# Routing of the last batch placed inside the expert block, expert weights in ten parts, a scan for the running sums

## The reference

```python
x = x + attn_a(norm(x))      # 16 heads, random features, and a dense feed-forward part
x = x + ffn(norm(x))         # 160 experts, the stage called m in the kernel
x = x + attn_b(norm(x))      # causal, 16 heads of 8, four sequences
x = x + ffn(norm(x))         # 160 experts again, the stage called n
...
# ffn, for every token
probs = sigmoid(x @ router_w.T + expert_bias)          # [T, 160]
top_w, top_idx = top_k(probs, 8)
top_w = 2.5 * top_w / (sum(top_w) + 1e-9)
combine[t, top_idx] = top_w
h1 = silu(einsum('th,eih->eti', x, w_gate))            # w_gate [160, 64, 128]
routed = einsum('eti,ehi->th', h1 * combine, w_down)   # w_down [160, 128, 64]
shared = silu(x @ w_gate_shared.T) @ w_down_shared.T
out = routed + shared
```

## Time and profile before

| | us |
|---|---|
| time before, median of 3 runs | 2836.28 |
| lowest and highest of them | 2828.25, 2845.3 |
| the profiled execution, its own time | 2840.0 |
| its span, first to last instruction | 2838.8 |
| around the span | 1.2 |
| mean granted TensorE clock | 0.806 of full |

### The profile page before, as it was taken

How to read it: one execution, slowest core, us unless ns; L and a number is a source line. 1 busy time by engine, 2 the same in 40 slices (tenths; PEclk the granted TensorE clock), 3 DMA queues, 4 the chain that set the end, 5 groups by cost and what they waited for, 6 DMA issues and landing times. The chain is left out here.

```text
span 2838.8 us, 45747 instructions
## 1 busy us (share of the span) xinstructions
PE 2002.9 (71%) x15915; PEld 1145.2 (40%) x15915; DVE 1632.1 (57%) x4701; ACT 1087.8 (38%) x2067; POOL 1264.2 (45%) x1244
## 2 busy tenths in 40 slices
PE   5898887877882775665878889888888467676000
PEld 3456455455461554542333333333342255454000
DVE  5457585784777231457776878688783533145222
ACT  0263453453540443440545544443444144444000
POOL 0043166566673444543434420430443444456775
PEclk8899989999995897885787878787887589878555
DMA  9200001000034664554132130121100656555221
GB/s 377 95 1 4 1 6 35 24 12 34 19 131 154 195 209 158 186 177 123 29 90 50 48 82 21 50 74 33 50 29 26 252 182 211 181 187 175 70 59 45
DMA packets 132475, 275.70 MB, mean 97 GB/s; under 512 B 29411, under 2 KB 44387, under 8 KB 127891
## 3 DMA queue, kind: packets, MB, share of 16 engines
q1 hardware_dynamic: 99478, 205.60, 21.8%
q0 software_dynamic: 32768, 67.17, 7.8%
HBM read 146.34 MB, written 125.93 MB: 96 GB/s over the span
## 5 line engine op out<-in xcount | busy, mean ns | idle before, releaser
L1473 POOL DMA_INDIRECT slots_in<-g_xs,g_place x512 | 508.5, 993 | 500.7 <-ACT b_pT L2521 188.6
L2521 ACT ACTIVATE b_pT<-b_psE 128x512 f32<-128x512 f32 (+3 forms) x768 | 330.4, 491 | 469.6 <-PE b_psE L2420 228.9
L2271 DVE TENSOR_REDUCE b_peak<-b_psM 128x1 f32<-128x512 f32 (+3 forms) x768 | 394.5, 551 | 141.5 <-PE b_psM L2403 87.0
L1498 POOL DMA_INDIRECT r_xs<-slots_out,g_place x336 | 333.0, 991 | 312.4 <-ACT b_pT L2521 183.3
L2400 PE MATMUL b_psM<-b_kS,b_qS 72*128 72x512 bf16 (+3 forms) x768 | 283.9, 402 | 66.2 <-DVE b_peak L2271 34.0
L2416 PE MATMUL b_psE<-b_qS,b_kS 75*128 75x512 bf16 (+3 forms) x768 | 258.5, 391 | 57.1 <-ACT b_pT L2521 39.5
L1498 POOL DMA_INDIRECT g_xs<-slots_out,g_place x176 | 172.4, 980 | 124.4 <-issue 48.1
L2060 DVE COPY m_staged_w<-wgd 128x192 f32 x512 | 98.3, 263 | 222.5 <-PE m_psY L2002 114.5
L2060 DVE COPY n_staged_w<-wgd 128x192 f32 x512 | 97.8, 262 | 207.7 <-PE n_psY L2002 147.8
L2430 PE MATMUL b_psV<-b_pT,b_vb 128*32 128x512 f32 (+3 forms) x1536 | 197.3, 597 | 2.5 <-ACT b_pT L2521 2.2
L2400 PEld LDWEIGHTS b_psM<-b_kS,b_qS 72*128 72x128 bf16 x768 | 83.5, 111 | 264.7 <-DVE b_peak L2271 138.6
(11 more groups left out here) (640 smaller groups left out, 4167.3 us busy)
## 6 DMA issues: line engine op xcount, KB each, us to landing
wgd<-in_w_gdT SPq DMA_DIRECT2D x8, 3840.0 KB, 23.0
slots_in<-g_xs SPq DMA_DIRECT2D x26, 1024.0 KB
m_rows<-slots_in SPq DMA_DIRECT2D x104, 256.0 KB
slots_out<-m_y SPq DMA_DIRECT2D x104, 256.0 KB
n_rows<-slots_in SPq DMA_DIRECT2D x104, 256.0 KB
slots_out<-n_y SPq DMA_DIRECT2D x104, 256.0 KB
b_qS<-q_parts SPq DMA_DIRECT2D x48, 192.0 KB
b_kS<-k_parts SPq DMA_DIRECT2D x48, 192.0 KB
```

Source lines behind the costliest of these rows:

```text
L1473: self.nc.gpsimd.indirect_dma_start(self.G.slots_in[self.h], bass.IndirectOffsetOnAxis(self.G.place[:, TPH * self.h + t, k:k + 1], 0), sel ...
L1498: self.nc.gpsimd.indirect_dma_start(self.rows(i)[:, k, :], None, self.G.slots_out[t // TPH], bass.IndirectOffsetOnAxis(self.G.place[:, t, ...
L2271: nc.vector.reduce_max(to, taking()[:, 0:size], AX.X).then_inc(m_taken, 1)
L2521: nc.scalar.activation(pT[:, e % KEPT, h, q0:HALF], psE[:, j % BANKS, q0:HALF], ACT.Exp, scale=SCALE).then_inc(e_taken, 1)
```

## The change

- `route` is gone. Its instructions for the last batch stand in `experts`, beside the 20 fixed groups of the first half. `Beside` says after which group each part of PE and ACT comes: in m (`LOADED_BESIDE_FFN`) turn after group 0, score 1, up 2, down 3, count 8, rank 9, owner 16; in n (`ALL_LOADED_HERE`) turn before group 0, score 0, up 1, down 2, count 3, rank 4, owner 10.
- DVE does the whole routing first, then waits for all weights, then begins to stage.
- The first half runs its 20 fixed groups first and its 32 dynamic ones after them (`static_first`; in m it begins with fixed group 10). The second half keeps `group_order`.
- While the routing uses the second psum banks, the fixed groups use the first one alone (`alone`), so `up(n)` waits for `squash(n-1)` and `down(n)` for `take_y(n-1)`.
- Buffers of the routing lie in the staging buffers (`Carved`).
- Weights come in 10 parts of 1.57 MB. In m five come during `ffn_a` and five beside groups 0, 2, 4, 6, 8. In n two come between the first four row loads and eight beside groups 0 to 14.
- POOL sends the rest of batch 2 at three transfers a group from the start, and then, once the slots are known (`placed`), batch 3 at two a group from group 19 on.
- The running sum is one `tensor_tensor_scan` in place of a copy and 8 doubling steps.

```diff
-CHUNKS = 4
+CHUNKS = 10
...
+def static_first(first):
+    return [((first + i) % STATIC_GROUPS, None) for i in range(STATIC_GROUPS)] + [(STATIC_GROUPS + d, d) for d in range(DYN_GROUPS)]
...
-def route(nc, stage, G, W, h, first, tiles, xn, xn_free=None, send=None, loads=None):
...
+LOADED_BESIDE_FFN = Beside(STATIC_GROUPS // 2, range(CHUNKS // 2), 0, 2, turn=0, score=1, up=2, down=3, count=8, rank=9, owner=16)
+ALL_LOADED_HERE = Beside(0, range(CHUNKS), 2, 2, turn=-1, score=0, up=1, down=2, count=3, rank=4, owner=10)
...
+        def alone(n):
+            return n < STATIC_GROUPS
...
+            def load_chunk(c):
+                e = slice(CHUNK * c, CHUNK * (c + 1))
+                sp.dma_start(G.wgd[:, e, :], W["w_gdT"][:, e, :]).then_inc(S.weights_landed[c], 16)
...
                 for i in range(DEEP):
-                    load(h, i)
+                    load(first + i)
+                    if h == 0 and i == 1:
+                        sp.dma_start(wr, W["routerT"]).then_inc(router_landed, 16)
...
+                    if h == 0 and 1 <= i <= beside.upfront:
+                        load_chunk(chunks.pop(0))
                 for i in range(HALF_GROUPS):
                     if i + DEEP < HALF_GROUPS:
-                        sp.wait_ge(x_turned, h * HALF_GROUPS + i + 1)
-                        load(h, i + DEEP)
-                    store(h, i)
+                        sp.wait_ge(x_turned, first + i + 1)
+                        load(first + i + DEEP)
+                    if chunks and i % beside.per == 0:
+                        load_chunk(chunks.pop(0))
+                    store(first + i)
...
-            spaced(scatter, TPH * TOPK - scatter.sent, 0, 3, 2)
+            scatter.upto = TPB * TOPK
+            spaced(scatter, TPB * TOPK - scatter.sent, 0, 3, 1)
+            scatter.of_batch(BATCH - 1)
+            pool.wait_ge(placed, 1)
+            spaced(scatter, TPB * TOPK, STATIC_GROUPS - 1, 2, 1)
...
+                if n and alone(n - 1):
+                    pe.wait_ge(hT_ready, n)
...
+                if n and alone(n - 1):
+                    pe.wait_ge(y_ready, n)
...
             for h in range(HALVES):
                 first = h * HALF_GROUPS
                 turn_rows(first)
-                for i, (g, d) in enumerate(order):
-                    up(first + i, g, d, h * DYN_GROUPS)
+                if h == 0:
+                    last_batch_at(-1)
+                for i in range(HALF_GROUPS):
+                    up(first + i)
                     if i + 1 < HALF_GROUPS:
                         turn_rows(first + i + 1)
                     if i:
-                        down(first + i - 1, *order[i - 1])
...
+                        down(first + i - 1)
+                    if h == 0:
+                        last_batch_at(i)
...
+            def last_batch_at(i):
+                if i == beside.turn:
+                    for u, ps in enumerate((bank0, bank1)):
+                        act.wait_ge(turned, u + 1)
+                        nc.scalar.activation(xnT[:, u * HALF:(u + 1) * HALF], ps, ACT.Copy).then_inc(xnT_ready, 1)
+                if i == beside.score:
+                    act.wait_ge(logits_taken, 1)
+                    nc.scalar.activation(probs, logits, ACT.Sigmoid).then_inc(probs_ready, 1)
+                if i == beside.up:
+                    for u, ps in enumerate(ups):
+                        act.wait_ge(up_shared, 2)
+                        nc.scalar.activation(hs[:, u * HALF:(u + 1) * HALF], ps[0:INTER, :], ACT.Silu).then_inc(hs_ready, 1)
...
-                step, now = 1, 0
-                while step < EXPERTS:
-                    nc.vector.tensor_copy(ends[:, 1 - now, 0:step], ends[:, now, 0:step])
-                    nc.vector.tensor_tensor(ends[:, 1 - now, step:], ends[:, now, step:], ends[:, now, 0:EXPERTS - step], ALU.add)
...
+                nc.vector.tensor_tensor_scan(ends, more, more, 0.0, ALU.add, ALU.max)
...
+            norm()
+            dve.wait_ge(made, 1)
...
+            add_bias()
+            choose()
+            for u in range(2):
+                add_shared(u)
+            plan()
+            find_places()
+            order_weights()
+            write_owners()
             for c in range(CHUNKS):
                 dve.wait_ge(S.weights_landed[c], 16)
             for d in range(DYN_GROUPS):
                 stage_weights(0, d)
+            dve.wait_ge(owners_written, 1)
...
-                route(nc, "m3_", G, W, *part(BATCH - 1), send, expert_loads(G, W, S["m"], range(CHUNKS // 2)))
-                send.of_batch(BATCH - 1)
-                experts(nc, "m", G, S["m"], send)
+                experts(nc, "m", G, W, S["m"], send, part(BATCH - 1), LOADED_BESIDE_FFN)
```

More of the change, by code:

```diff
@@ L1892, in experts, with __init__ @@
-def experts(nc, stage, G, S, scatter, out=None):
+class Beside:
+    def __init__(self, first_group, chunks, upfront, per, turn, score, up, down, count, rank, owner):
+        self.first_group, self.chunks, self.upfront, self.per = first_group, list(chunks), upfront, per
+        self.turn, self.score, self.up, self.down, self.count, self.rank, self.owner = turn, score, up, down, count, rank, owner
+LOADED_BESIDE_FFN = Beside(STATIC_GROUPS // 2, range(CHUNKS // 2), 0, 2, turn=0, score=1, up=2, down=3, count=8, rank=9, owner=16)
@@ L1896, in experts @@
+def experts(nc, stage, G, W, S, scatter, last_batch, beside, out=None):
+    h_last, first_tile, tiles, xn, xn_free = last_batch
+    assert tiles == TPB and first_tile == TPB and h_last == HALVES - 1
     with Memory(nc, stage) as m:
@@ L1927, in _ @@
             for h in range(HALVES):
+                first = h * HALF_GROUPS
                 for b in range(BPH * h, BPH * (h + 1)):
@@ L1949, in spaced @@
                 for n in range(0, count, transfers):
-                    done = min(n // transfers * groups, HALF_GROUPS)
+                    done = min(n // transfers * groups, HALF_GROUPS - first % HALF_GROUPS)
                     if done:
@@ new lines, in count, with rank @@
+            def count():
+                pe.wait_ge(made, 3)
+                pe.wait_ge(picked_ready, 1)
+                nc.tensor.matmul(counts, ones_bf, before[:, TPB, :], start=True, stop=True).then_inc(counted, 1)
+            def rank():
+                pe.wait_ge(share_ready, 1)
+                pe.wait_ge(shared_taken, 2)
+                for tiles_here, ps in rank_tiles:
+                    if tiles_here.stop == TPB:
+                        pe.wait_ge(count_taken, 1)
+                    for i, t in enumerate(range(tiles_here.start, tiles_here.stop)):
+                        nc.tensor.matmul(ps[:, i, :], earlier, picked[:, t, :], start=True, stop=False)
+                        nc.tensor.matmul(ps[:, i, :], ones_bf, before[:, t, :], start=False, stop=False)
+                        last = nc.tensor.matmul(ps[:, i, :], ones_bf[0:1, :], share[:], start=False, stop=True)
+                last.then_inc(ranked, 1)
@@ new lines, in turn_owner @@
+            def turn_owner():
+                pe.wait_ge(owner_ready, 1)
+                pe.wait_ge(rank_taken, 1)
+                for i in range(OWNERS):
+                    last = nc.tensor.matmul(owners[:, i * P:(i + 1) * P], owner[:, i:i + 1], G.ident[:], start=True, stop=True)
+                last.then_inc(owner_turned, 1)
+            def last_batch_at(i):
+                if i == beside.turn:
+                    turn_last_batch()
+                if i == beside.score:
+                    score()
+                if i == beside.up:
+                    up_of_shared()
+                if i == beside.down:
+                    down_of_shared()
+                if i == beside.count:
+                    count()
+                if i == beside.rank:
+                    rank()
+                if i == beside.owner:
+                    turn_owner()
```

588 lines of the change are left out of this document (250 added, 338 removed).

## The result

The changed kernel took 2815.1 us, the median of six runs (2804.2 to 2821.5), against 2837.1 for the kernel before (six runs, 2828.3 to 2845.3). The ratio is 0.9926, with a 95% interval of 0.9898 to 0.9954. It is faster by 22 us, where 72 were forecast, and lies outside the range. That of before is 2.9 above its own.

What follows compares the result with a forecast made beforehand. DVE's serial chain was taken to bound the routing blocks, and PE's loop the groups. Terms of -42.3 us in m and -30.2 in n took 2840.0 to 2767.5; the stated median was 2765, the 8-in-10 range 2745 to 2800.

Steps and rivals of the forecast that it cites:

- Staging: First halves' 32 dynamic groups in a row: DVE's staging takes 2.1 us against 2.98 a group, so it costs nothing.
- Routing beside the groups, +18 and +16: First halves' fixed groups: the routing work of PE and ACT adds 18 us in m and 16 in n.
- parts, +2 and +4: Weight parts loaded beside the fixed groups: mostly absorbed by rows asked for ahead, costing 2 us in m and 4 in n.
- The round trip of ACT: After the scores, ACT waits for DVE's bias, then does a table load and sigmoid before the next squash: 4.0 us exposed.
- +3.7 for `up(0)` in n: Start of n: group 0 needs weight part 0, so its up starts at about 9.5 us in place of 5.8.
- Gap between m's halves, -8.4: Between m's halves: row copies start in time, so the gap of 8.9 us shrinks to n's 0.5.
- Slots known at 65 and 52 us: Batch 3's slots known 65 us into the block in m and 52 in n, before group 19's result at some 83.
- Bounds: Whole kernel: 2745 us with full clock for PE's parts (-11), DMA absorbed and ACT's trip half hidden; 2814 the other way.
- The first: Rival: DMA bounds the fixed groups, late rows stopping the loop; +17 over the terms, 2782 us; chance 0.14.
- The second: Rival: each of PE's routing parts stops the loop, which starts anew; +30, 2795 us; chance 0.13.
- The third: Rival: slots known only after group 31, so copies end 35 us after the last result; 2835 us; chance 0.03.
- Staging (0.04): Rival: staging bounds the dynamic groups in a row; slower by over 0.5% from 4.35 us a group; chance 0.04.

Runs made afterwards that it cites:

- e2: Changed kernel with the last batch's 64 row copies moved behind the first half's last result; with its three repeats 2709 to 2721 us, before at 2607 to 2613.
- e4: Kernel before with the changed kernel's order in the first halves, fixed groups first and then 32 dynamic ones, copies still three for two groups; ratio 0.9990 to before.
- e14: Changed kernel with the last batch's copies released from the 12th result on in place of the 20th; ratio 0.9800 to before.
- e13: Changed kernel with n's last eight weight parts asked for one to a group in place of one to two groups; ratio 0.9855 to before.

## Why the prediction was wrong

**The failed step is the cost of the row copies beside the groups.** The prediction put it as "At two per group they need 2.5 us of 2.98", a claim on POOL's time alone, and under Staging as "Nothing": 2.98 us was kept as the pace of a dynamic group, while the change raises the rate from 1.5 copies a group to 2. Measured in the comparison: the dynamic groups of m carried 62 copies where before's last 32 groups carried 48, and took 15.0 us longer; those of n carried 62 in place of 42 and took 16.9 longer. That is 1.07 and 0.85 us for each copy more, near the 0.96 for which a copy keeps POOL busy. The row that said so stood in the prediction's own material: the second halves, with two gathers a group, take 191 us for 52 groups in the earlier trace rows, 3.48 each in n between first and last result, where the first halves take 2.98. I read their length as given and never asked why a group costs half a microsecond more there.

Behind it stands a count that I left out. The routing block hid 20 copies a stage (20.60 us of POOL in the earlier trace rows). When the block goes, they move beside the groups, in n all of them beside the dynamic ones. In the sum they were free.

**How firmly this stands.** That order and staging are not the cause is shown by e2 and its repeats and by e4, at the lower level. For the comparison it rests on its own traces: PE never waits for DVE in the dynamic groups, and before runs fixed groups at 2.9 to 3.0 us with DVE idle. That copies beside the loop lengthen it is shown at both levels: in the comparison by before's groups with three copies and with none, at the same granted clock, and at the lower level by 2.0 us without copies and 2.1 to 2.4 with them. That they account for all of the 15.0 and 16.9 us is argued, from the pace at three rates; no experiment met that level. The granted clock is a rival for a part. It stood at 0.75 in m's dynamic groups, and PE's busy time grew there from 68.9 to 76.2 us, so up to 7.3 of the 15.0 could be the clock's, unless the clock fell because PE stood still. In n the busy time grew by only 2.0 of 16.9 us. Nor is it settled how a copy stops TensorE's results from coming out, or what makes a copy cost 0.4 to 1.1 us at one level and 0.1 to 0.2 at the other.

**The sum by its other steps.**
- *Serial block removed, -107.8*: right, rows are loaded at the start of both stages.
- *Routing beside the groups, +18 and +16, and parts, +2 and +4*: near as a sum at the comparison's level, 3.5 and 4.5 us too low. That it came out is partly luck: in m 39 copies stood between the first and the 20th result where before had 27, at a clock of 0.77 against 0.94, and neither was in the terms. The shares can be told apart at the lower level only, and are off there: routing with some copies 13 and 11, parts 9 and 21. The prediction priced the parts against a pair of groups of 5.96 us; a pair of 4.0 hides less. The round trip of ACT, put at 4.0, took 6.0 in m and 6.7 in n from its first table load to the next squash; a second table load, before the sigmoid, was left out.
- *+3.7 for `up(0)` in n*: it starts at +10.5 us (9.5 forecast, though the three terms given for it add up to 8.05). The 5.8 of before is m's; in n `up(0)` started at 4.5, so the term is 6.0. The first result comes 10.2 us later than before's, as ACT waits for the scores and takes the sigmoid, with its two table loads, ahead of it. That is part of the 16.
- *Gap between m's halves, -8.4*: right, -7.8.
- *Slots known at 65 and 52 us*: 66.9 and 50.8. But POOL then waited for the 20th result, 16.8 us in m, and this waste the prediction counted as "in time". At the lower level e14 takes it back in n.
- *Scan*: one pass over 160 elements took 0.49 us, where the copy of the same shape took 0.24, as the Trainium skill's page "DVE: opcode table, instruction layouts, handler registers and perf-mode slots" (section "Datapath and trigger behaviour") let expect with half throughput; by this the trace agrees. It moved nothing.
- *DMA share near 1 in n up to the 16th group*: it was 0.85 up to the 20th result; e13 shows that the parts can be asked for sooner.
- *Bounds*: full clock for PE's parts takes the two terms from 13 + 11 to 9 + 9, which is -6 and not -11, so the lower bound was 2750 by its own terms. The measured time lies above the range, and nothing hangs on it.
- *Rest of batch 2's copies in 51 us in m*: they are let out with the results, and the last started 74.7 us into the stage (932.97), after the slots were known.

**The rivals.** The first (parts as the bound, 0.14) is wrong for the comparison: in n PE waited 5.9 us for parts and 1.4 for rows after its first group, and the first 20 groups leave no room for 17 more. It is right for n at the lower level. The second (interleaving costs 30 more, 0.13) has no room either, with 3.5 and 4.5 us over the terms. The third (slots known too late, 0.03) is out with 66.9 and 50.8 us. Staging (0.04) named the right place, the dynamic groups, and a wrong mechanism; its threshold of 3.5 us, given as the sign of being wrong altogether, was nearly met with 3.45 and 3.39. No rival said that a copy costs the loop something.

## What to carry to other kernels

When serial work is taken away, count what ran hidden beside it, here 20 copies a stage, and price it at its new place. Work on an engine that isn't the bottleneck can still set the pace of the others: compare two stretches of the same loop that differ in it alone, as the two halves did here, before its cost is put at nothing. And when such work must go beside the loop, start it as soon as its inputs are known and stretch it over all groups that are left.

## What was not expected of the hardware

The same kernel, with the same instructions, has taken 2828 to 2845 us in one set of runs and 2600 to 2626 in five others. The profiles differ mostly where indirect copies run beside TensorE's loop: 2.98 against 2.13 us a group at three copies for two groups, 3.4 against 2.3 at two gathers a group, and 1.96 (two groups) against 1.99 without any. The last stretch, in which POOL gathers and TensorE does nothing, is not shorter but 8 us longer at the lower level (213.8 and 221.8). At the slower level results of matmuls of 1.12 us came out some 3 us late while four copies were issued in a row. Which of the two levels one is on seems to decide what a change to the copies is worth: at one the changed kernel gained 0.7%, at the other 1.3%, with intervals that just touch.
